# Causal attention whose keys lie on partitions: maxima taken from PSUM, row sums as products with ones, reciprocals in a small tile, z copied out at once, one PSUM ring for the rest

## The reference

```python
x = x + attention(layernorm(x))     # x: 2048 rows of 128, 16 heads of 64
# attention:
scores = jnp.einsum('biph,biqh->biqp', K, Q)
scores = jnp.where(tril, scores, NEG_INF)
attn = softmax(scores / sqrt(64), axis=-1)
z = jnp.einsum('biph,biqp->biqh', V, attn)
out = jnp.einsum('bqf,df->bqd', z_flat, W_O)
```

## Time and profile before

| what | value |
| --- | --- |
| time, median of 2 runs | 1825.82 us (1824.38 to 1827.26) |
| the profiled execution | 1830.6 us, its span 1828.8 us |
| mean granted TensorE clock | 0.806 of full speed |
| busy in the span: DVE, PE, POOL, ACT | 1460.3, 1248.3, 998.6, 772.4 us |
| attention's own busy lines, DVE: sum, max, reciprocal | L343 452.7, L321 428.1, L346 107.3 us |

### The profile page before, as it was taken

How to read it: one execution, slowest core, us unless ns; L and a number is a source line. 1 busy time by engine, 2 the same in 40 slices (tenths; PEclk the granted TensorE clock), 3 DMA queues, 4 the chain that set the end, 5 groups by cost and what they waited for, 6 DMA issues and landing times. The chain is left out here.

```text
span 1828.8 us, 17099 instructions
## 1 busy us (share of the span) xinstructions
PE 1248.3 (68%) x5632; PEld 737.6 (40%) x5632; DVE 1460.3 (80%) x1516; ACT 772.4 (42%) x1168; POOL 998.6 (55%) x494
## 2 busy tenths in 40 slices
PE   5376767686767676767667776767686654688636
PEld 4243444343434443334434343433353134634436
DVE  4399799978897888889798879897989863569735
ACT  4254454444344534543454345534454322432224
POOL 0147674577448743965294629473847724445243
PEclk9698789787878787889787878987887656879768
DMA  6900100000000000000000000000000001200013
GB/s 127 162 0 1 35 12 1 12 23 12 1 23 12 12 1 23 12 12 1 23 12 12 1 23 12 12 0 24 12 12 1 0 0 49 73 2 0 1 48 91
DMA packets 48556, 40.71 MB, mean 22 GB/s; under 512 B 14177, under 2 KB 41442, under 8 KB 48482
## 3 DMA queue, kind: packets, MB, share of 16 engines
q1 hardware_dynamic: 45922, 34.50, 8.7%
q0 software_dynamic: 2560, 5.26, 0.9%
HBM read 13.49 MB, written 9.48 MB: 13 GB/s over the span
## 5 line engine op out<-in xcount | busy, mean ns | idle before, releaser
L286 POOL TENSOR_TENSOR at_kept<-at_kept,at_shift 128x1024 f32<-128x1024 f32 (+1 forms) x320 | 856.2, 2714 | 615.1 <-ACT at_shift L406 615.1
L401 ACT ACTIVATE at_kept<-at_ring 128x1024 f32<-128x1024 f32 (+1 forms) x320 | 283.2, 896 | 603.6 <-PE at_ring L476 263.8
L343 DVE TENSOR_TENSOR at_esum<-at_esum,at_kept 128x1024 f32<-128x1024 f32 (+3 forms) x264 | 452.7, 1715 | 5.6
L321 DVE TENSOR_TENSOR at_peak<-at_peak,at_kept 128x1024 f32<-128x1024 f32 (+3 forms) x264 | 428.1, 1621 | 20.6 <-ACT at_kept L401 14.9
L507 PE MATMUL at_z<-at_kept,at_v 128*64 128x512 f32 (+3 forms) x1280 | 354.6, 655 | 57.9 <-ACT at_kept L411 57.5
L473 PE MATMUL at_ring<-at_q_st,at_k_st 128*128 128x512 f32 (+3 forms) x640 | 282.1, 441 | 139.9 <-ACT at_kept L401 97.6
L411 ACT ACTIVATE at_kept<-at_kept 128x1024 f32<-128x1024 f32 (+1 forms) x320 | 290.2, 925 | 91.1 <-POOL at_kept L286 90.7
L476 PE MATMUL at_ring<-at_q_st,at_k_st 128*128 128x512 f32 (+3 forms) x640 | 268.3, 419 | 0.0
L473 PEld LDWEIGHTS at_ring<-at_q_st,at_k_st 128*128 128x128 f32 x640 | 135.7, 212 | 313.1 <-ACT at_kept L401 175.8
L507 PEld LDWEIGHTS at_z<-at_kept,at_v 128*64 128x64 f32 x1280 | 79.0, 156 | 209.2 <-issue 108.0
L346 DVE RECIPROCAL at_rinv<-at_o 128x512 f32<-128x512 f32 x32 | 107.3, 3353 | 58.6 <-PE at_o L515 58.3
(11 more groups left out here) (194 smaller groups left out, 1505.4 us busy)
## 6 DMA issues: line engine op xcount, KB each, us to landing
at_q_st<-at_q_st SPq DMA_DIRECT2D x64, 256.0 KB, 3.7
f_xs<-slots_in SPq DMA_DIRECT2D x48, 64.5 KB, 1.9
slots_in<-zeros SPq DMA_DIRECT2D x2, 1536.0 KB, 18.4
wall<-in_L_ffn_w_dram SPq DMA_DIRECT2D x1, 2048.0 KB, 18.7
wall<-in_L_ffn_w_dram SPq DMA_DIRECT2D x4, 512.0 KB, 6.3
f_got<-slots_out SPq DMA_DIRECT2D x8, 256.0 KB, 3.6
out_dram<-x SPq DMA_DIRECT2D x4, 256.0 KB, 2.4
slots_out<-f_ys,f_back POOLq DMA_INDIRECT x48, 2.2
```

The costliest lines, as they stand in the source:

```text
L286: pool.tensor_tensor(rows, rows, shift[g % 2][:, :, skip(g, t):BANK], ALU.add).then_inc(s_sub, 1)
L321: dve.tensor_tensor(some, some, rows, ALU.max).then_inc(s_max, 1)
L343: dve.tensor_tensor(some, some, rows, ALU.add).then_inc(s_sum, 1)
L401: act.activation(scores_of(g, t), ring[use_of[("score", g, t)] % RING][:, :, 0:w], ACT.Copy).then_inc(s_kept, 1)
```

## The change

- `max` reads the scores from the ring's PSUM bank (after keep has read it too) instead of from `at_kept`. Each chunk's first unit is now copied to `at_peak`, where before the maximum of units 0 and 1 was taken in one instruction. A score's bank is free for PE when DVE's `max` has read it, where before it was free after `keep`.
- `sum` moves from DVE to PE: two units at a time are multiplied by a 128 x 32 tile of ones, each of the four products (two tiles, two heads) on 32 columns of the array of its own, and added up in the new bank `at_l`. In the first chunk of a pair both tiles use the same columns. `total` and `esum` are gone.
- At a chunk's end ACT copies `at_l` to SBUF (`lsum`), PE transposes it (`norm`), DVE reduces it to 8 sums a partition and takes 8 reciprocals, PE spreads these (`spread`, eight products), and DVE multiplies (`leave`).
- `zraw` (DVE) copies z out of its bank at once, so that the next chunk's `value` waits for that and no longer for `leave`.
- `norm` and `spread` share one bank of the ring, held from `norm` to `leave`; `out` takes another, held to `add`. The bank `at_o` is gone.
- The plan's assumed lengths, ranks and penalties are changed, and with them the orders.

```diff
-        step(("keep", g, t), "act", 0.16 + 0.73 * part, ("pe", "score", g, t), held and ("pe", "value") + held, held and ("dve", "sum") + held)
+        step(("keep", g, t), "act", 0.18 + 0.85 * part, ("pe", "score", g, t), held and ("pe", "value") + held,
+             held and ("pe", "sum", held[0], held[1] // 2))
-        step(("sub", g, t), "pool", 0.2 + 1.9 * part, ("act", "shift", g))
+        step(("sub", g, t), "pool", 0.3 + 2.05 * part, ("act", "shift", g))
-        step(("sum", g, t), "dve", 0.08 + 1.07 * part, ("act", "exp", g, t),
-             g and ("pe", "total", g - 1))
+        if t % 2:
+            step(("sum", g, t // 2), "pe", 0.87 * (part + (t >= tiles(g) - TPC) * P / BANK), ("act", "exp", g, t), g and ("act", "lsum", g - 1))
...
-        step(("total", g), "dve", 0.65, ("pe", "total", g))
-        step(("leave", g), "dve", 0.65, ("dve", "total", g), ("pe", "value", g, end), g > 1 and ("pe", "out", g - 2))
+        step(("zraw", g), "dve", 0.7, ("pe", "value", g, end))
+        step(("lsum", g), "act", 0.6, ("pe", "sum", g, end // 2))
+        step(("norm", g), "pe", 0.45, ("act", "lsum", g))
+        step(("norm", g), "dve", 0.5, ("pe", "norm", g))
+        step(("spread", g), "pe", 0.87, ("dve", "norm", g))
+        step(("leave", g), "dve", 0.7, ("pe", "spread", g), ("dve", "zraw", g), g > 1 and ("pe", "out", g - 2))
...
-    reader = {"score": ("act", "keep"), "turn": ("dve", "peak"), "shift": ("act", "shift"), "project": ("dve", "low"), "vproject": ("act", "vproject")}
+    reader = {"score": ("dve", "max"), "turn": ("dve", "peak"), "shift": ("act", "shift"), "project": ("dve", "low"),
+              "vproject": ("act", "vproject"), "norm": ("dve", "leave"), "out": ("dve", "add")}
...
+                        bank = ring[use_of[("score", g, t)] % RING][:, :, 0:width(g, t)]
...
-                        some = top[:, :, skip(g, t):BANK]
-                        dve.tensor_tensor(some, some, rows, ALU.max).then_inc(s_max, 1)
+                        some = peak[g % 2][:, :, skip(g, t):BANK]
+                        dve.tensor_tensor(some, bank, some, ALU.max).then_inc(s_max, 1)
...
-                        dve.reciprocal(rinv[:, :], o_ps[:, :]).then_inc(s_rinv, 1)
+                        dve.tensor_reduce(total[:, :, :], rows[:, :, :, 0:parts, 0], AX.X, ALU.add).then_inc(s_total, 1)
                         dve.wait_ge(s_total, g + 1)
+                        dve.reciprocal(rinv[:, :, :], total[:, :, :]).then_inc(s_rinv, 1)
...
+                    elif kind == "sum":
+                        if it[2] == 0 and g >= 1:
+                            pe.wait_ge(s_lsum, g)
+                        pe.wait_ge(s_exp, unit(g, 2 * it[2] + 1) + 1)
+                        for t in (2 * it[2], 2 * it[2] + 1):
+                            b = t % 2 if g % NC else 0
+                            for h in range(2):
+                                part = slice((2 * b + h) * P // 4, (2 * b + h + 1) * P // 4)
+                                last = pe.matmul(l_ps[part, skip(g, t):BANK], ones[:, :], scores_of(g, t)[:, h, :],
+                                                 start=t == 0 or (b == 1 and t == 1), stop=t == tiles(g) - 1 or (g % NC > 0 and t == tiles(g) - 2))
+                        last.then_inc(s_sum, 1)
```

More of the change, by code:

```diff
@@ L106, in attention_plan @@
         step(("turn", g), "pe", 0.9, ("dve", "max", g, end))
-        step(("peak", g), "dve", 1.15, ("pe", "turn", g))
+        step(("peak", g), "dve", 1.25, ("pe", "turn", g))
         step(("shift", g), "pe", 1.75, ("dve", "peak", g))
-        step(("shift", g), "act", 0.9, ("pe", "shift", g), g > 1 and ("pool", "sub", g - 2, tiles(g - 2) - 1))
-        step(("total", g), "pe", 0.87, ("dve", "sum", g, end), g and ("dve", "add", g - 1), ("pe", "value", g, end))
-        step(("total", g), "dve", 0.65, ("pe", "total", g))
-        step(("leave", g), "dve", 0.65, ("dve", "total", g), ("pe", "value", g, end), g > 1 and ("pe", "out", g - 2))
+        step(("shift", g), "act", 1.05, ("pe", "shift", g), g > 1 and ("pool", "sub", g - 2, tiles(g - 2) - 1))
+        step(("zraw", g), "dve", 0.7, ("pe", "value", g, end))
[4 more added lines that the diff above has]
+        step(("leave", g), "dve", 0.7, ("pe", "spread", g), ("dve", "zraw", g), g > 1 and ("pe", "out", g - 2))
         step(("out", g), "pe", 0.88, ("dve", "leave", g))
-        step(("add", g), "dve", 0.65, ("pe", "out", g))
+        step(("add", g), "dve", 0.7, ("pe", "out", g))
         step(("project", g), "pe", 1.75, g > 1 and ("pe", "score", g - 2, tiles(g - 2) - 1),
@@ L121, in attention_plan @@
             step(("vproject", p, c), "pe", 0.95, p and ("pe", "value", NC * p - 1, 8 * c + 7))
-            step(("vproject", p, c), "act", 0.9, ("pe", "vproject", p, c))
-    reader = {"score": ("act", "keep"), "turn": ("dve", "peak"), "shift": ("act", "shift"), "project": ("dve", "low"), "vproject": ("act", "vproject")}
[L126 to L129, removed]
+            step(("vproject", p, c), "act", 1.05, ("pe", "vproject", p, c))
+    reader = {"score": ("dve", "max"), "turn": ("dve", "peak"), "shift": ("act", "shift"), "project": ("dve", "low"),
+              "vproject": ("act", "vproject"), "norm": ("dve", "leave"), "out": ("dve", "add")}
+    urgent = {"pe": ["turn", "shift", "norm", "spread", "out", "vproject", "same", "project", "other"],
+              "act": ["shift", "lsum", "vproject", "high", "keep"],
+              "dve": ["peak", "zraw", "norm", "leave", "add", "low", "max"], "pool": ["sub"], "sp": ["second"]}
+    column_tiles = {"value": 2, "spread": 2, "sum": 4}
     def rank(s, since, last):
-        kind = equal.get(s[1], s[1])
-        if s[0] == "pe" and kind == "score":
-            kind = "same" if s[1] == last else "score"
+        kind = "keep" if s[1] == "exp" else s[1]
+        if kind in ("score", "value", "sum"):
+            kind = "same" if kind == last else "other"
         return urgent[s[0]].index(kind), since, s[2:]
@@ L155, in attention_plan @@
             if e == "pe":
[L156 removed]
+                length += 0.17 * (column_tiles.get(s[1]) != column_tiles.get(last))
                 last = s[1]
@@ L179, in attention @@
     order, tiles, skip, width, first_unit, place, before = attention_plan(PAIRS, NC, TPC)
-    uses = [it for it in order["pe"] if it[0] in ("score", "turn", "shift", "project", "vproject")]
+    uses = [it for it in order["pe"] if it[0] in ("score", "turn", "shift", "project", "vproject", "norm", "out")]
     use_of = {it: n for n, it in enumerate(uses)}
-    reads = {"score": 0, "turn": 0, "shift": 0, "project": 0, "vproject": 0}
+    reads = {"score": 0, "turn": 0, "shift": 0, "project": 0, "vproject": 0, "norm": 0, "out": 0}
     reader = []
@@ L325, in _ @@
                                           AX.X, ALU.max, negate=True).then_inc(s_low, 1)
[L326 to L337, removed]
-                            else:
-                                dve.tensor_copy(esum[:, :, :], rows).then_inc(s_sum, 1)
-                            continue
-                        dve.wait_ge(s_sum, unit(g, t))
-                        some = esum[:, :, skip(g, t):BANK]
-                        dve.tensor_tensor(some, some, rows, ALU.add).then_inc(s_sum, 1)
-                    elif kind == "total":
+                    elif kind == "zraw":
+                        dve.wait_ge(s_value, first_unit[g + 1])
+                        if g >= 1:
+                            dve.wait_ge(s_zT, g)
+                        dve.tensor_copy(zraw[:, :], z_ps[:, :]).then_inc(s_zraw, 1)
+                    elif kind == "norm":
+                        dve.wait_ge(s_normT, g + 1)
+                        parts = 1 if g % NC == 0 else 2
+                        rows = ring[use_of["norm", g] % RING][:, 0, :].rearrange("p (i b h r) -> p i h b r", i=TPC, b=2, h=2)
+                        dve.tensor_reduce(total[:, :, :], rows[:, :, :, 0:parts, 0], AX.X, ALU.add).then_inc(s_total, 1)
```

77 lines of the change are left out of this document (46 added, 31 removed).

## The result

The changed kernel takes 1533.46 us (1532.33 to 1534.6, 2 runs) against 1825.82: the ratio is 0.8399, 95% interval 0.836 to 0.8438. The profiled execution took 1532.3 us, 298.3 less than the 1830.6 before.

A forecast was written before the change was run, and what follows sets the result against it. DVE bounds before, PE after: 129 us of work, 3.6 idle and 7.4 for the clock make 140 us a pair. Savings of 249, 20 and 13 us leave 1548.6 of 1830.6; less 4.8, the median is 1544 us, range 1460 to 1690.

The forecast's parts named there:

- What bounded before: Unit loop of the kernel before: DVE bounds, busy 155 of 177 us a pair (88%).
- The prices: Busy time of each engine for one pair after the change: PE 129 us, ACT 86, POOL 80, DVE 68.
- Four products side by side: PE's sum step, four products on 32 columns each: priced as a value's 1.01 us plus 0.1 for a change of form.
- The 11 us on top of PE's work: Per pair beyond PE's 129 us: 3.6 us idle at the last chunk and 7.4 for two falls of the clock.
- The ring costs nothing: Score banks in a full unit: held 3.6 us, three give a unit every 1.2 us where PE needs 2.7.
- DVE stops being the bound even at the upper end: DVE's load for one pair after the change: 68 us, at most 92 if maxima were stretched, against 155.
- The sum: Whole kernel: seven periods save 249 us, the first chunks 20, the last chunk 13, in all 282 us.
- four products run as two and two: Rival on PE's sum steps: 14 us more a pair, 154 us, 1650 us in all; chance 0.10.
- a clock that stays at 0.85: Rival on PE's granted clock: no rise from today's, 155 us a pair, 1657 us in all; chance 0.15.
- The chain at a chunk's end: Two rivals, lsum to add uncovered: 164 us a pair, chance 0.08; with the ring empty too, 188 us, chance 0.04.
- POOL's wait before a pair's last chunk: Sign in the unit loop: POOL waits near 10 us there, reckoned as 10.4, against 32 us before.
- The waits that were to refute it: PE's waits for `at_rinv`, `at_zraw` or the banks' readers: more than 10 us a pair would show the prediction wrong.

The follow-up runs named there:

- e2: Kernel before with only the maxima reading PSUM and a score's bank free after them; sums stay on DVE: 1641.7 us, ratio 0.897.
- e1: Changed kernel with maxima reading SBUF again and a score's bank free after ACT's copy; sums stay on PE: 1632.0 us, ratio 0.893.
- e11: Changed kernel with maxima reading SBUF again, its orders and its rule for freeing banks kept: 1631.2 us, ratio 0.890.
- e3: Changed kernel with both tiles of a sum step on the same columns, so two products run at a time, orders unchanged: 1622.4 us.
- e6: Changed kernel with one more reciprocal of 512 values a partition on DVE after each chunk's add: 1583.8 us, ratio 0.864.
- e8: Changed kernel with the shift products in fp32r instead of fp32 and the plan's length for them 0.9: 1504.3 to 1528.8 us.

## Why the prediction was right, by its own steps

**What bounded before.** Right. DVE at 88% was the bound, and freeing it by either half gives 185 to 200 us (e2, e1).

**The prices.** PE 129 us a pair was measured as 129.4, DVE 68 as 67.8, ACT 86 as 85.7, POOL 80 as 80.8. The maxima from PSUM were priced from the reduction, 1.21 us, and take 1.22; zraw and leave 0.69, as assumed; sub 2.36 became 2.40. The two small instructions take 0.17 and 0.20 us for an assumed 0.25. The rule of the Trainium skill that fits is in "GPSIMD Engine Reference", section Key points: GpSimd contends for SBUF with VectorE instructions that have two SBUF inputs or run in a 2-port mode. The trace agrees: with PSUM as one input a maximum is 1.22 us, in e1 with two from SBUF 2.20.

**Four products side by side.** The step takes 1.00 us where a value's two take 1.01; it was priced at 1.1 with a change of form. The factor of 2.38 for three column tiles, which the prediction cites from the Trainium skill ("TensorE: Matmul & The Clock Gate"), would have made it 0.2 us dearer by its estimate; the trace shows nothing of that, and the measurement decides.

**The 11 us on top of PE's work.** The size was right (10.4), its parts were not. I expected 3.6 us of idle time and 7.4 lost to a falling clock. PE waited 10.3 us, for DVE's steps at a chunk's end and for ring banks, and the clock was 0.99: it fell once, to 0.81 from 957 to 966 behind out's wait of 2.4 us, 1.7 us by the prediction's own way of reckoning. (That way gives 3.4 us a fall from its own row, where the prediction put 3.7.) The idle time it reckoned was of another kind, too. POOL's stall before a pair's last chunk is 14 us, for 10.4 reckoned, and the one before the third chunk, which the prediction left out, is 33 us; yet no value in the window waits for exp, so PE covers both with other work. The period hit 140 by luck: too much for the clock and too little for the waits met at the same size.

**The ring costs nothing.** Wrong as put. Bank time against PE's pace (1.2 against 2.7 us) is an average, and the cost is in single stalls: 2.3 us a pair for scores behind maxima and 2.4 for shift behind its bank even in the changed kernel, 5.7 more when DVE has 13.4 more to do, 15.5 more with two banks and their order. In the same way "DVE stops being the bound even at the upper end" was true and not enough: stretched maxima would have cost 10 to 12 us a pair (e1, e11), 98 us in all, though no engine would have been full.

**The sum.** Seven periods gave 250.6 for 249. Up to the first pair's last chunk it was 30.9 for 20: that start moved from 201.0 to 170.1, 7.0 of it before POOL's second chunk, which I held to be bound by DMAs alone, and 23.9 after. From the last pair's last chunk on it was 16.7 for 13: POOL's 46.2 became 33.9, and the rest 4.3 shorter. Together 298.2 for 282, so the profiled execution came 16 us below the 1548.6 forecast for it. The medians are only 10 apart (1533.5 for 1544), because the forecast took off 4.8 for the gap between profiled and median run of before, while the median after lies 1.1 above its profiled run. Why the start gained 31 us instead of 20 was not looked into.

**The rivals.** That four products run as two and two is excluded by e3, a clock that stays at 0.85 by the 0.99 above. The chain at a chunk's end shows with 3.9 us a pair (out and spread), 5.6 with `zraw`, not 24 or 48. Of the signs set out beforehand all came but one: POOL's wait before a pair's last chunk is 14 us and not near 10. The waits that were to refute it, for `at_rinv`, `at_zraw` and the banks' readers, come to 1.5 + 1.7 + 4.7 = 7.9 us, not far under the 10 named.

## What to carry to other kernels

Price an operation by a row that has its kind of operands, on a stretch where its neighbour works: PSUM with SBUF for PSUM with SBUF. When the bounding engine is freed, sum up every engine's list for one period at its undisturbed prices; the largest sum was within 8% of the new period here. Then ask of each engine whose instructions release a resource what a single late one costs, for here an engine at half load passed on 43% of what was added to it (e6).

## What the runs showed that I had not expected

- Two halves that each give 185 to 200 us give 292 together, not 385: with the maxima alone DVE is still the bound (89% in e2), and with the rest alone DVE's and POOL's stretched instructions make PE wait (e1, e11).
- Contention cost more by latency than by load: in e1 it adds 32 us of DVE and 18 us of POOL time a pair, on engines that have room for it, and 10 us show. Freeing the banks otherwise (e11) didn't remove them but moved them from value and turn to the scores.
- With e8's order single executions of one kernel on one chip differ by up to 25 us, in step with the mean granted clock (0.898 to 0.918), where the changed kernel's five differ by 3 (0.924 to 0.927). What sets it was not tried.
